# First attention of a two-layer kernel: value projection of one head in full float32 against two heads per product in three rounded passes

## The chip, the cores and the metric

The kernel runs on 1 core of one Trainium2 chip. The metric is the device time of one execution in microseconds (us); the median of several runs is compared.

## The reference, cut to what matters

Two transformer layers over 4 x 256 tokens of width 256; the case is about the first operation, an attention of 16 heads of 128:

```python
q = split_heads(x @ Wq); k = split_heads(x @ Wk); v = split_heads(x @ Wv)
q = _apply_rope(q, cos, sin); k = _apply_rope(k, cos, sin)
scores = einsum('bhqd,bhkd->bhqk', q, k) / sqrt(HD)      # causal mask, softmax
ctx = einsum('bhqk,bhkd->bhqd', attn, v)
return ctx @ Wo
```

After it come a layer norm, a decay scan, a mixture of experts with 32 experts, and the second layer (attention, gated linear attention, experts). Everything is float32.

## The kernel before, in words

Sizes: T = 1024 tokens (B = 4 sequences of S = 256, NT = 8 tiles of 128), D = 256 (DC = 2 chunks of 128 rows), H = 16 heads, HD = 128. The program of each engine is written out by hand; engines meet only at semaphores, and each engine executes its own list strictly in order.

`layer0_attention` (lines 346 to 611) treats one head per round, `heads(emit)`, and in a round the four sequences b = 0..3. Beside the attention of head h, TensorE projects head h + 1. `CHUNKS` names the six projection jobs of a head: q and k and v, each for two halves of 512 tokens; `BESIDE = {0: (0, 1), 1: (2, 3), 2: (4, 5), 3: ()}` puts q0 and k0 into round b = 0, v0 and q1 into b = 1, k1 and v1 into b = 2, nothing into b = 3. All jobs use two PSUM banks in turn (`proj_ps[:, c % 2]`), so each job waits until the job two before it has been read out: a q or k job by VectorE's `rotate_in` (line 488 multiplies by the cosine, line 492 shuffles neighbouring rows; semaphore rot_in), a v job by ScalarE's `keep_v` (line 572; semaphore v_kept).

- q and k jobs go through `product` (lines 72 to 78): weights and tokens are cut into a rounded float32r high part and a low part, and three matmuls (high x low, high x high, low x high) stand for one float32 matmul. The high part of a head's weights is made by ScalarE in `cut_high` (line 578, at b = 0 of head h for head h + 2), the low part by GpSimd in `cut_low` (line 552), for head 1 by VectorE (line 507). x_h and x_l, the two parts of the tokens, are made once (lines 583 and 499).
- A v job (line 434) is 4 token tiles x 2 chunks = 8 plain float32 matmuls of 128 columns, with k.xT (the tokens, float32) as the stationary operand and the head's 128 columns of Wv moving.

TensorE's order in a round of b: the scores of (h, b) (lines 326 and 327), the projection jobs of that b, the transposes of the softmax of two rounds ago (line 265, waits for VectorE's `divide`, lines 297 to 300, semaphore normed), and probabilities times values of three rounds ago (lines 274 and 275). VectorE's order: maxima (line 334), the `rotate_in` of the jobs of this b, `divide` of the round before. ScalarE's order: `exps` (lines 340, 342), `cut_high` if b = 0, `keep_turned` (line 306), `keep_mixed` (line 313), `keep_v`. GpSimd's order per head: `cut_low` for head h + 2 (two operations), then four `rotate`s for head h + 1, each a multiplication by the sine (line 543) and an addition (line 547; semaphore rotated). The scores of b = 0 wait until GpSimd has finished q0 and k0 of their head, those of b = 2 until it has finished q1 and k1.

SyncE loads Wq, Wk and Wv of a head together, 128 KB each (line 395), two heads ahead; the load of head h waits for the v jobs of head h - 2. `load_rest` (constants) and `load_tail` (k.x, the token-major copy of x, 1 MB, and Wo, 2 MB) stand between the loads of heads 1, 2 and 3. k.x is first read in `layer0_tail` (line 759), after the attention.

Of the kernel before, what the change touches and what calls it, by code (L numbers as in the profile page):

```python
# [41 lines left out]
class Memory:  # L42
# [6 lines left out]
    def sb(self, name, shape, dt=F32):  # L49
        return self.stack.enter_context(self.nc.sbuf_tensor(name, shape, dt))  # L50

# [294 lines left out]
def layer0_attention(nc, k, I):  # L346

    with ExitStack() as stack:
        m = Memory(nc, stack)
        ROT = 4  # L350
        w = m.sb("a0_w", [P, 2, 3, DC, HD])
        w_p = Parts(m, "a0_w", [P, 2, 2, DC, HD])
        x_h, x_l = m.sb("a0_x_h", [P, DC, T], F32R), m.sb("a0_x_l", [P, DC, T], F32R)
        qk = m.sb("a0_qk", [P, 2, 2, T])
        v = m.sb("a0_v", [P, 2, NT, HD])
# [8 lines left out]
        w1_low = m.sem("a0_w1_low")  # L364
        w_in = [m.sem("a0_w_in0"), m.sem("a0_w_in1")]
        qk_proj = m.sem("a0_qk_proj")
# [11 lines left out]
        NQK = {0: 1, 1: 2, 3: 3, 4: 4}  # L378
        NV = {2: 1, 5: 2}
# [9 lines left out]
        with nc.Block() as block:  # L389
            @block.sync  # L390
            def _(sp):
                def load(h, par):
                    at_least(sp, v_proj, 2 * (h - 2) + 2)
                    for n, name in enumerate(("L0_attn_Wq", "L0_attn_Wk", "L0_attn_Wv")):
                        sp.dma_start(w[:, par, n], I[name][:, h * HD:(h + 1) * HD].rearrange("(c p) d -> p c d", p=P)
                                     ).then_inc(w_in[par], 16)
                load(0, 0)
                load(1, 1)
                load_rest(sp, k, I)
                load(2, 0)  # L400
# [12 lines left out]
            @block.tensor  # L413
            def _(pe):
                def project(h, pair, par, c):
                    what, half = CHUNKS[c]
                    if what == "v":
                        pe.wait_ge(w_in[par], 48 * (pair + 1))
                    else:
                        if h == 1:  # L420
                            pe.wait_ge(w1_low, PIECE[what] + 1)
                        else:
                            pe.wait_ge(w_low, 2 * max(h - 1, 0) + PIECE[what] + 1)
                    if h == 0:
                        pe.wait_ge(x_low, DC * (half + 1))
                    prev, prev_h = (c - 2, h) if c >= 2 else (c + 4, h - 1)
                    if prev in NQK:
                        at_least(pe, rot_in, 4 * prev_h + NQK[prev])
                    else:
                        at_least(pe, v_kept, 2 * prev_h + NV[prev])  # L430
                    if what == "v":
# [5 lines left out]
                        last.then_inc(v_proj, 1)  # L437
                    else:
                        tokens = slice(half * HALF, (half + 1) * HALF)
                        for kc in range(DC):  # L440
                            last = product(pe, proj_ps[:, c % 2, :], w_p[:, par, PIECE[what], kc, :],
                                           (x_h[:, kc, tokens], x_l[:, kc, tokens]), kc == 0, kc == DC - 1)
                        last.then_inc(qk_proj, 1)

                def mix(h, par, b):
                    if b % 2 == 0:
                        pe.wait_ge(v_kept, 2 * h + b // 2 + 1)
                    at.mix(pe, 4 * h + b, b, lambda j: v[:, par, 2 * b + j, :])
# [3 lines left out]
                for c in range(len(CHUNKS)):  # L452
                    project(0, 0, 0, c)
                pe.wait_ge(k.first_in, k.n_first)

                def emit(h, pair, par, first, last, ahead):
                    for b in range(B):
# [4 lines left out]
                        if not last:  # L462
                            for c in BESIDE[b]:
                                project(h + 1, pair + par, 1 - par, c)
# [15 lines left out]
            def _(dve):  # L480
                def rotate_in(h, c):
                    what, half = CHUNKS[c]
                    count = 4 * h + NQK[c]
                    r = NQK[c] - 1
# [4 lines left out]
                                      proj_ps[:, c % 2, :].rearrange("p (b s) -> p b s", b=2),  # L489
                                      cos[:, None, :].to_broadcast([P, 2, S]), ALU.mult)  # L490

                    dve.stream_shuffle(swapped[:, r, :], proj_ps[:, c % 2, :], [i ^ 1 for i in range(32)]  # L492
# [9 lines left out]
                for c in NQK:  # L502
                    rotate_in(0, c)
# [17 lines left out]
                def emit(h, pair, par, first, last, ahead):  # L521
                    for b in range(B):
                        n = 4 * h + b
                        at.maxima(dve, n, b)
                        if not last:
                            for c in BESIDE[b]:
                                if c in NQK:
                                    rotate_in(h + 1, c)
# [2580 lines left out]
```

## Time and profile before

| | us |
|---|---|
| median of 3 runs | 1132.42 (1131.62 to 1134.52) |
| span of the profiled execution | 1133.0 |
| first projection matmul (q0 of head 0) | at 10.61 |
| scores of head 0 begin | at 20.57 |
| scores of head 15 (the last) begin | at 260.11 |
| output projection of the attention begins | at 276.26 |
| TensorE busy in the span | 1029.7 (91%) |
| VectorE, ScalarE, GpSimd busy | 732.4 (65%), 574.6 (51%), 466.2 (41%) |

Times in the trace are us from the start of the span. PE is TensorE's matmuls, PEld its weight loads, DVE VectorE, ACT ScalarE, POOL GpSimd. A matmul's bar begins when it starts and overlaps the next one, so what a matmul costs is read from the start of one to the start of the next. A float32 matmul stands in the trace as two records, a float32r matmul as one.

### The profile page before, as it was taken

Reading aid. Unit: us, or ns where it says so; the run is one execution under the profiler, and the core shown is the slowest. Engines: PE = TensorE matmul, PEld = TensorE weight load, DVE = VectorE, ACT = ScalarE, POOL = GpSimd, SP = SyncE. Lnnn points to the kernel's source line nnn. Section 1 sums busy time; section 2 is a strip of 40 time slices with the busy share of each in tenths; the row PEclk is TensorE's granted clock in tenths of the full one; section 3 lists DMA queues with packets and bytes.
Section 4 is the critical chain, followed back from the end, with each engine's and each line's share of the span. In section 5 each row is a group of like instructions: output and inputs, shape, how many; then the busy total and the mean of one; then the engine's idle time right before and its main releaser. Section 6 shows DMA issues by size and latency. Waiting matters only on the chain. (4 is left out here: it accounts for less than half of the span.)

```text
span 1133.0 us, 18735 instructions
## 1 busy us (share of the span) xinstructions
PE 1029.7 (91%) x5986; PEld 825.7 (73%) x5986; DVE 732.4 (65%) x2146; ACT 574.6 (51%) x1568; POOL 466.2 (41%) x481
## 2 busy tenths in 40 slices
PE   8999999998995699579899999988978889999995
PEld 5888888887873699547778888845444568877784
DVE  5988887883675366446656672126686657788875
ACT  3454555445221355346667772037875546655553
POOL 5777777861277344455111110010135313444322
PEclk9999999999997899879999999988998989999998
DMA  6631111000011799626101101001003011112101
GB/s 217 235 132 61 29 30 28 19 12 1 1 54 56 237 354 333 196 69 186 37 25 61 30 15 38 1 21 50 2 1 114 0 56 56 57 56 75 38 1 38
DMA packets 83495, 85.59 MB, mean 76 GB/s; under 512 B 8545, under 2 KB 75943, under 8 KB 83280
## 3 DMA queue, kind: packets, MB, share of 16 engines
q1 hardware_dynamic: 79056, 75.39, 20.4%
q0 software_dynamic: 3072, 7.34, 2.2%
q10 hardware_dynamic: 1280, 1.77, 0.5%
q8 instruction: 46, 0.75, 0.3%
q14 instruction: 41, 0.34, 0.1%
HBM read 63.36 MB, written 22.02 MB: 75 GB/s over the span
## 5 line engine op out<-in xcount | busy, mean ns | idle before, releaser
L547 POOL TENSOR_TENSOR a_qk<-h,a_by_sin 128x512 f32<-128x512 f32 x64 | 86.6, 1353 | 5.0
L334 DVE CUSTOM_DVE_ANT_0 h<-a_score_ps,mask_bf 128x128 f32<-128x128 f32 (+1 forms) x128 | 40.7, 355 | 62.0 <-PE a_score_ps L327 62.0
L306 ACT ACTIVATE a_probsT<-a_turn_ps 128x384 f32<-128x384 f32 x128 | 61.3, 479 | 36.1 <-PE a_turn_ps L265 36.1
L1265 POOL TENSOR_TENSOR a_w_l<-a_w,a_w_h 128x256 fp32r<-128x256 f32 x30 | 21.8, 727 | 113.1 <-ACT a_w_h L1458 112.9
L340 ACT ACTIVATE y_moe<-y_moe,a_nmax 128x128 f32<-128x128 f32 x64 | 25.7, 402 | 82.8 <-DVE a_nmax L334 82.5
L434 PEld LDWEIGHTS a_proj_ps<-a_w,xT 128*128 128x128 f32 x512 | 62.0, 192 | 3.2 <-issue 1.2
L434 PE MATMUL a_proj_ps<-a_w,xT 128*128 128x128 f32 x512 | 62.5, 275 | 0.4 <-DVE hT L492 0.4
L1004 POOL TENSOR_TENSOR e_w_l<-e_w,e_w_h 128x512 fp32r<-128x512 f32 x32 | 40.9, 1278 | 52.3 <-ACT e_w_h L1072 52.3
L76 PE MATMUL a_proj_ps<-a_x_l,a_w_h 128*128 128x512 f32 x128 | 55.8, 436 | 2.6 <-ACT a_v L572 0.8
L728 PE MATMUL t_y_ps<-wo,attnT 128*128 128x256 f32 x256 | 57.6, 381 | 0.0
L2513 POOL TENSOR_TENSOR m_up_l<-m_up_w,m_up_h 128x1024 fp32r<-128x1024 f32 x8 | 19.5, 2434 | 89.4 <-ACT m_up_h L2485 89.4
L1505 PE MATMUL p_y_ps<-wo,attnT 128*128 128x256 f32 x256 | 55.5, 379 | 0.8 <-PEq L1237 0.8
L299 DVE TENSOR_SCALAR y_moe<-y_moe,a_rtotal 128x128 f32<-128x128 f32 x64 | 53.4, 835 | 2.3
L1505 PEld LDWEIGHTS p_y_ps<-wo,attnT 128*128 128x128 f32 x256 | 48.6, 190 | 7.5 <-issue 0.9
L728 PEld LDWEIGHTS t_y_ps<-wo,attnT 128*128 128x128 f32 x256 | 47.7, 190 | 6.0
L78 PE MATMUL a_proj_ps<-a_x_h,a_w_l 128*128 128x512 f32 x128 | 50.4, 394 | 0.0
L340 ACT ACTIVATE h<-h,a_nmax 128x128 f32<-128x128 f32 x64 | 25.7, 402 | 48.2 <-DVE a_nmax L334 48.2
L77 PE MATMUL a_proj_ps<-a_x_h,a_w_h 128*128 128x512 f32 x128 | 50.0, 390 | 0.0
L492 DVE STREAM_SHUFFLE hT<-a_proj_ps 128x512 f32<-128x512 f32 x64 | 47.2, 737 | 0.0
L334 DVE CUSTOM_DVE_ANT_0 y_moe<-a_score_ps,mask_bf 128x128 f32<-128x128 f32 (+1 forms) x128 | 40.2, 349 | 9.7 <-PE a_score_ps L327 9.6
L543 POOL TENSOR_TENSOR a_by_sin<-hT,sin_k 128x512 f32<-128x512 f32 x32 | 41.2, 1287 | 10.0 <-DVE hT L492 10.0
L1997 DVE TENSOR_TENSOR wo<-l_dec,l_qk_ps 128x384 f32<-128x384 f32 x64 | 35.2, 550 | 15.6 <-ACT l_dec L1960 14.1
(439 smaller groups left out, 3373.6 us busy)
## 6 DMA issues: line engine op xcount, KB each, us to landing
slots<-zeros SPq DMA_DIRECT2D x4, 2048.0 KB, 7.1
e_rows<-slots SPq DMA_DIRECT2D x32, 256.0 KB, 4.7
e_w<-in_L_ffn_w_dram SPq DMA_DIRECT2D x32, 256.0 KB, 4.9
out_slots<-e_out SPq DMA_DIRECT2D x32, 256.0 KB, 4.3
e_w<-in_L_ffn_w_dram SPq DMA_DIRECT2D x32, 128.0 KB, 4.3
a_w<-in_L_attn_w_q_dram SPq DMA_DIRECT2D x32, 128.0 KB, 2.3
m_up_w<-in_up_dram SPq DMA_DIRECT2D x8, 512.0 KB, 3.8
a_w<-in_L_attn_Wq_dram SPq DMA_DIRECT2D x16, 128.0 KB, 2.3
```

The lines of the kernel that those rows point to most:

```text
L76: pe.matmul(out, left[0], right[1], start=start, stop=False)
L77: pe.matmul(out, left[0], right[0], start=False, stop=False)
L78: return pe.matmul(out, left[1], right[0], start=False, stop=stop)
L299: dve.tensor_scalar(self.probs[:, b, 0:P], self.probs[:, b, 0:P], self.rtotal[:, b, 0:1], None, ALU.mult)
L306: act.activation(self.probsT[:, b % 2, :], self.turn_ps[:, b % 2, 0:CAUSAL], ACT.Copy).then_inc(self.turned_kept, 1)
L334: done = dve.tensor_tensor_reduce(self.probs[:, b, cells], self.score_ps[:, r, cells], self.k.mask_bf[:, cells], -1.0, 3e38, ALU.add, ALU. ...
L340: act.activation(self.probs[:, b, 0:P], self.probs[:, b, 0:P], ACT.Exp, bias=self.nmax[:, b, 0:1], scale=-1.0, accum_out=self.total[:, b, ...
L434: last = pe.matmul(proj_ps[:, c % 2, t * HD:(t + 1) * HD], k.xT[:, kc, half * HALF + t * P:half * HALF + (t + 1) * P], w[:, par, 2, kc, :] ...
L492: dve.stream_shuffle(swapped[:, r, :], proj_ps[:, c % 2, :], [i ^ 1 for i in range(32)]).then_inc(rot_in, 1)
L547: pool.tensor_tensor(qk[:, par, 0 if what == "q" else 1, half * HALF:(half + 1) * HALF], by_cos[:, r, :], by_sin[:, r2, :], ALU.add).then_ ...
L728: last = pe.matmul(y_ps[:, t % 2, 0:D], k.ctxT[:, h, t * P:(t + 1) * P], k.wo[:, h, :], start=h == 0, stop=h == H - 1)
L1505: last = pe.matmul(y_ps[:, t % 2, 0:D], k.ctxT[:, h, t * P:(t + 1) * P], k.wo[:, h, :], start=h == 0, stop=h == H - 1)
```

## The change

Values are no longer projected per head but per group of two heads (VG = 2, eight groups). A value job is now a quarter of the tokens (two tiles of 128) for 256 columns of Wv, in float32r parts, three matmuls for each tile and chunk: 2 x 2 x 3 = 12 matmuls of 256 columns. There are four such jobs per group, two beside each head, at the places where the value jobs stood; the group of heads 2g and 2g + 1 is projected beside heads 2g - 2 and 2g - 1. All four jobs of group 0 stand in the opening, ahead of the first scores; beside head 14 there are no value jobs. The second value buffer is k.xT, which nothing else reads after the opening; the parts of Wv lie in k.x, so the load of k.x moves behind the last value job. The cuts of Wv come with it: one 128x512 operation of ScalarE and one of GpSimd per group (of VectorE for group 1), for groups 2 to 7 in the odd heads 1 to 11, ScalarE's after `exps` of b = 1, GpSimd's between `cut_low` and the first `rotate`. SyncE loads Wv in 256 KB pieces into a single buffer, each after the cut of the piece before it.

```diff
-        w = m.sb("a0_w", [P, 2, 3, DC, HD])
+        w = m.sb("a0_w", [P, 2, 2, DC, HD])
+        wv = m.sb("a0_wv", [P, DC, VG * HD])
+        wv_h, wv_l = (m.at(f"a0_wv_{n}", [P, 2, DC, VG * HD], k.x_at + i * 8 * DC * VG * HD, F32R)
+                      for i, n in enumerate("hl"))
-        v = m.sb("a0_v", [P, 2, NT, HD])
+        v = [m.sb("a0_v", [P, NT, VG * HD]), k.xT[:, :, :].rearrange("p c (t w) -> p (c t) w", w=VG * HD)]
...
-        CHUNKS = [("q", 0), ("k", 0), ("v", 0), ("q", 1), ("k", 1), ("v", 1)]
-        BESIDE = {0: (0, 1), 1: (2, 3), 2: (4, 5), 3: ()}
+        OPENING = [("q", 0, 0), ("k", 0, 0), ("v", 0, 0), ("q", 0, 1), ("k", 0, 1), ("v", 0, 1), ("v", 0, 2), ("v", 0, 3)]
+        def beside(h, b):
+            if h == H - 1:
+                return []
+            g = h // VG + 1
+            values = [("v", g, 2 * (h % VG) + i) for i in range(2)] if g < GROUPS_V else [None, None]
+            jobs = {0: [("q", h + 1, 0), ("k", h + 1, 0)], 1: [values[0], ("q", h + 1, 1)],
+                    2: [("k", h + 1, 1), values[1]], 3: []}[b]
+            return [job for job in jobs if job]
...
             def _(sp):
                 def load(h, par):
-                    at_least(sp, v_proj, 2 * (h - 2) + 2)
-                    for n, name in enumerate(("L0_attn_Wq", "L0_attn_Wk", "L0_attn_Wv")):
+                    at_least(sp, qk_proj, 4 * (h - 2) + 4)
+                    for n, name in enumerate(("L0_attn_Wq", "L0_attn_Wk")):
...
+                def load_v(g):
+                    if g:
+                        low_of(sp, g - 1)
+                    sp.dma_start(wv[:, :, :], I["L0_attn_Wv"][:, g * VG * HD:(g + 1) * VG * HD
+                                                              ].rearrange("(c p) d -> p c d", p=P)).then_inc(wv_in, 16)
                 load(0, 0)
+                load_v(0)
                 load(1, 1)
+                load_v(1)
                 load_rest(sp, k, I)
                 load(2, 0)
-                load_tail(sp, k, I)
+                load_v(2)
+                load_wo(sp, k, I)
                 for h in range(3, H):
                     load(h, h % 2)
+                    if h % VG and (h + 3) // VG < GROUPS_V:
+                        load_v((h + 3) // VG)
...
+                sp.wait_ge(v_proj, B * GROUPS_V)
+                load_x(sp, k, I)
...
-                        for t in range(NT // 2):
-                            for kc in range(DC):
-                                last = pe.matmul(proj_ps[:, c % 2, t * HD:(t + 1) * HD],
-                                                 k.xT[:, kc, half * HALF + t * P:half * HALF + (t + 1) * P],
-                                                 w[:, par, 2, kc, :], start=kc == 0, stop=kc == DC - 1)
+                        for t in range(QT):
+                            cells = slice((QT * i + t) * P, (QT * i + t + 1) * P)
+                            for kc in range(DC):
+                                last = product(pe, out[:, t * VG * HD:(t + 1) * VG * HD],
+                                               (x_h[:, kc, cells], x_l[:, kc, cells]),
+                                               (wv_h[:, of % 2, kc, :], wv_l[:, of % 2, kc, :]), kc == 0, kc == DC - 1)
...
             def _(dve):
+                dve.wait_ge(wv_high, 2)
+                dve.tensor_tensor(wv_l[:, 1], wv[:, :, :], wv_h[:, 1], ALU.subtract).then_inc(wv1_low, 1)
...
             def _(pool):
+                def cut_values(g):
+                    pool.wait_ge(wv_high, g + 1)
+                    pool.tensor_tensor(wv_l[:, g % 2], wv[:, :, :], wv_h[:, g % 2], ALU.subtract).then_inc(wv_low, 1)
                 cut_low(0, 0)
+                cut_values(0)
...
                     if ahead:
                         cut_low(h + 2, par)
+                    if par and (h + 3) // VG < GROUPS_V:
+                        cut_values((h + 3) // VG)
...
             def _(act):
+                def cut_values(g):
+                    act.wait_ge(wv_in, 16 * (g + 1))
+                    at_least(act, v_proj, B * (g - 1))
+                    act.activation(wv_h[:, g % 2], wv[:, :, :], ACT.Copy).then_inc(wv_high, 1)
...
                         if b == 0 and ahead:
                             cut_high(h + 2, pair + 1, par)
+                        if b == 1 and par and (h + 3) // VG < GROUPS_V:
+                            cut_values((h + 3) // VG)
```

A job's bank is now its number in the whole order modulo 2, and it waits for the read-out of the job two before it, as before. In the opening ScalarE cuts the first head's q and k weights once Wq and Wk have landed (it waited for all three matrices), then Wv of group 0, then the second half of the tokens. The product itself keeps its place and its lines move by four (81, 80 and 82 answer to 77, 76 and 78).

## Rows read from the trace of the kernel before

**Rows 1.** The page: busy share of PE; granted TensorE clock in 40 slices.

```profile
PE 1029.7 (91%) x5986; PEld 825.7 (73%) x5986; DVE 732.4 (65%) x2146; ACT 574.6 (51%) x1568; POOL 466.2 (41%) x481
...
PEclk9999999999997899879999999988998989999998
```

**Rows 2.** Busy time by engine of heads 14, 15 and 7.

```profile
core 0: us, PE busy (x) PEld busy (x) DVE busy (x) ACT busy (x) POOL busy (x), PEclk, DMA share, GB/s
...
243.71:260.11 16.40, 15.90 (x103) 14.00 (x102) 14.45 (x40) 7.68 (x26) 10.44 (x9) 1.00 0.01 1
260.11:273.30 13.19, 10.68 (x64) 8.41 (x62) 6.39 (x34) 9.87 (x36) 0.00 (x0) 1.00 0.00 0
131.00:147.11 16.11, 15.99 (x103) 13.93 (x101) 13.27 (x41) 8.49 (x29) 11.93 (x11) 1.00 0.09 25
```

**Rows 3.** Groups of instructions, first 330 us: busy us, mean ns, idle before.

```profile
L434 PE MATMUL a_proj_ps<-a_w,xT 128*128 128x128 f32 x512 | 62.5, 275 | 0.4 <-DVE hT L492 0.4
...
L299 DVE TENSOR_SCALAR y_moe<-y_moe,a_rtotal 128x128 f32<-128x128 f32 x64 | 53.4, 835 | 2.3
...
L552 POOL TENSOR_TENSOR a_w_l<-a_w,a_w_h 128x256 fp32r<-128x256 f32 x30 | 21.3, 731 | 48.3 <-ACT a_w_h L578 48.2
```

**Rows 4.** Timeline of head 7, PE (start us, length us, engine, line, operation).

```profile
131.00 0.39 PE L326 MATMUL a_score_ps<-a_qk 128*128 128x128 f32 x2
...
136.07 1.95 PE L434 MATMUL a_proj_ps<-a_w,xT 128*128 128x128 f32 x16
...
137.77 0.48 PE L76 MATMUL a_proj_ps<-a_x_l,a_w_h 128*128 128x512 f32 x1
...
142.63 1.95 PE L434 MATMUL a_proj_ps<-a_w,xT 128*128 128x128 f32 x16
...
144.41 0.49 PE L265 MATMUL a_turn_ps<-ident,y_moe 128*128 128x128 f32 x3
...
147.11 0.39 PE L326 MATMUL a_score_ps<-a_qk 128*128 128x128 f32 x2
```

**Rows 5.** Timeline of the first experts, PE, float32r products of 256 columns.

```profile
391.42 0.28 PE L76 MATMUL e_up_ps<-e_rowsT_l,e_w_h 128*128 128x256 f32 x1
...
392.14 1.03 PE L1045 MATMUL e_down_ps<-e_w,e_actT 128*128 128x256 f32 x4
```

**Rows 6.** Timeline of head 7, around TensorE's two waits.

```profile
139.44 0.69 DVE L488 TENSOR_TENSOR h<-a_proj_ps,cos_q 128x512 f32<-128x512 f32 x1 [1.77 <-PE a_proj_ps L78]
...
140.41 0.60 ACT L572 ACTIVATE a_v<-a_proj_ps 128x512 f32<-128x512 f32 x1
...
141.13 0.19 PEld L76 LDWEIGHTS a_proj_ps<-a_x_l,a_w_h 128*128 128x128 f32 x1 [0.50 <-issue]
...
144.39 1.36 DVE L299 TENSOR_SCALAR y_moe<-y_moe,a_rtotal 128x128 f32<-128x128 f32 x1
...
145.68 0.34 DVE L300 TENSOR_SCALAR y_moe<-y_moe,a_rtotal 128x256 f32<-128x256 f32 x1
...
146.07 0.31 PEld L265 LDWEIGHTS a_turn_ps<-ident,y_moe 128*128 128x128 f32 x3 [0.26 <-DVE y_moe L300]
```

**Rows 7.** Timeline of head 7, POOL, and ScalarE where the new cut goes.

```profile
134.11 1.42 POOL L552 TENSOR_TENSOR a_w_l<-a_w,a_w_h 128x256 fp32r<-128x256 f32 x2 [3.08 <-ACT a_w_h L578]
...
135.49 1.27 POOL L543 TENSOR_TENSOR a_by_sin<-hT,sin_q 128x512 f32<-128x512 f32 x1
...
139.76 0.49 ACT L306 ACTIVATE a_probsT<-a_turn_ps 128x384 f32<-128x384 f32 x1 [1.08 <-PE a_turn_ps L265]
...
145.75 1.40 POOL L547 TENSOR_TENSOR a_qk<-h,a_by_sin 128x512 f32<-128x512 f32 x1
```

**Rows 8.** Timeline of the opening.

```profile
9.34 0.72 ACT L578 ACTIVATE a_w_h<-a_w 128x256 fp32r<-128x256 f32 x2 [1.71 <-DMA a_w<-in_L_attn_Wv_dram]
...
10.61 0.50 PE L76 MATMUL a_proj_ps<-a_x_l,a_w_h 128*128 128x512 f32 x1 [0.38 <-POOL a_w_l L552]
...
20.57 0.30 PEld L326 LDWEIGHTS a_score_ps<-a_qk 128*128 128x128 f32 x2
```

More of the change, by code:

```diff
@@ L411, in _, with free @@
                                                                        k.zeros.shape[1]])).then_inc(k.zeroed, 16)
+                sp.wait_ge(v_proj, B * GROUPS_V)
+                load_x(sp, k, I)
             @block.tensor
             def _(pe):
-                def project(h, pair, par, c):
-                    what, half = CHUNKS[c]
+                def free(job):
+                    n = number[job]
+                    if n < 2:
+                        return
+                    what, of, i = order[n - 2]
@@ L417, in project @@
                     if what == "v":
-                        pe.wait_ge(w_in[par], 48 * (pair + 1))
+                        pe.wait_ge(v_kept, B * of + i + 1)
                     else:
[L420 to L426, printed above, removed]
@@ L427, in project @@
[L427 to L443 removed]
+                        pe.wait_ge(rot_in, 4 * of + COUNT[what, i])
@@ L461, in emit @@
                                   lambda i, j: qk[:, par, 1, b * S + i:b * S + j])
-                        if not last:
-                            for c in BESIDE[b]:
-                                project(h + 1, pair + par, 1 - par, c)
+                        for job in beside(h, b):
+                            project(job)
                         if b >= at.TURN or not first:
@@ L480, in _, with rotate_in @@
             def _(dve):
[L481 to L484, printed above, removed]
+                def rotate_in(job):
+                    what, h, half = job
+                    count = 4 * h + COUNT[what, half]
+                    r = COUNT[what, half] - 1
                     dve.wait_ge(qk_proj, count)
@@ L501, in _ @@
                 dve.wait_ge(k.first_in, k.n_first)
-                for c in NQK:
-                    rotate_in(0, c)
+                for job in OPENING:
+                    if job[0] != "v":
+                        rotate_in(job)
                 for piece in range(2):
@@ L524, in emit @@
                         at.maxima(dve, n, b)
[L525 to L528, printed above, removed]
+                        for job in beside(h, b):
+                            if job[0] != "v":
+                                rotate_in(job)
                         if b or not first:
@@ L536, in _, with rotate @@
             def _(pool):
[L537 to L540 removed]
+                def rotate(h, what, half, par):
+                    count = 4 * h + COUNT[what, half]
+                    r, r2 = COUNT[what, half] - 1, COUNT[what, half] % 2
                     sin = k.sin_q if what == "q" else k.sin_k
@@ L585, in _ @@
                         cut_high(0, 0, 0)
+                        cut_values(0)
                 cut_high(1, 0, 1)
-                for c in NV:
-                    keep_v(0, 0, c)
+                keep_v(0, 0)
+                keep_v(0, 1)
+                cut_values(1)
+                keep_v(0, 2)
+                keep_v(0, 3)
                 def emit(h, pair, par, first, last, ahead):
@@ L599, in emit @@
                             at.keep_mixed_act(act, n - at.KEEP, b, h - 1)
-                        if not last:
-                            for c in BESIDE[b]:
-                                if c in NV:
-                                    at_least(act, at.mixed, 4 * h - 2 + 2 * CHUNKS[c][1])
-                                    keep_v(h + 1, 1 - par, c)
+                        for job in beside(h, b):
+                            if job[0] == "v":
+                                keep_v(job[1], job[2])
                 heads(emit)
@@ L2991, in build @@
         k = Shared()
+        k.x_at = -(-nc.sbuf_base // 32) * 32
         k.x = m.sb("x", [P, NT, D])
```

82 lines of the change are left out of this document (57 added, 25 removed).

## The prediction

> **What bounds the kernel now.** I read the page first: TensorE is busy for 91% of the span and its granted clock is near full throughout [rows 1]. An average says nothing of one stage, so next the busy times of one head of the first attention, head 7, from its first scores to those of head 8: 16.11 us, of which PE 15.99, DVE 13.27, POOL 11.93, ACT 8.49, at a granted clock of 1.00, the 2.4 GHz level [rows 2]. TensorE bounds this stage, with VectorE and GpSimd not far behind. The timeline of that head then shows where TensorE still stands. Its weight loads pause twice: 0.50 us ahead of k1, which needs the bank that ScalarE's `keep_v` frees (140.41 + 0.60 = 141.01, k1's load at 141.13), and 0.26 us ahead of the transposes of b = 3, which need VectorE's `divide` (145.68 + 0.34 = 146.02, load at 146.07) [rows 6]. All else in the head is TensorE's own list.
>
> **TensorE, beside a head.** Removed: two value jobs of 16 records (512 in all, as the group's count says [rows 3]). The job in b = 1 runs from 136.07 to the start of q1 at 137.77, 1.70 us; that first q1 matmul is about 0.08 longer than its fellows since it follows float32 work, so the job is worth 1.78. The one in b = 2 runs from 142.63 to 144.41, 1.78 us [rows 4]. Added: two jobs of 12 float32r matmuls of 256 columns. The expert stage has just this form, also with the stationary operand changed each time: six of them from 391.42 to 392.14, so 0.72 / 6 = 0.120 us each [rows 5], and a job is 12 x 0.120 = 1.44 us. The saving is 1.78 - 1.44 = 0.34 us a job, 0.68 a head. The matmul count rises by half, the columns per head by as much, but one pass per column replaces the two records of 0.111 us.
>
> How much of it reaches the clock on the wall is a matter of the two waits. The wait ahead of k1 follows the transposes of b = 1 through ScalarE (`keep_turned` at 139.76, `keep_mixed`, `keep_v` at 140.41 [rows 6, 7]); when the job before those transposes is shorter, the whole chain moves, and the wait stays as it is: 0.34 kept. The job in b = 2 stands beside another chain: from the end of q1 VectorE works without a gap, from the first multiplication at 139.44 to the end of `divide` at 146.02 [rows 6], and only then can TensorE transpose. If VectorE takes as long as now, the 0.34 of this job turns into a longer wait. But in this chain two `divide` operations (line 299) last 1.36 us where the group's mean is 0.835 [rows 3, 6]: GpSimd's operations run at the same time. The Trainium skill (SBUF — State Buffer, the single rule) says that VectorE and GpSimd share a port pair under an exclusive lock, held for a whole instruction; the 1.36 us, as long as one GpSimd operation, agree, and by that rule a shifted GpSimd changes each `divide`. GpSimd does shift here (next paragraph), so VectorE's chain hits other phases of it, and the two collisions are already about the worst there are. Bounds per head: 0.34 (VectorE's chain as long as now) and 0.68 + 0.26 = 0.94 (the chain so much shorter that the second wait goes too). I take 0.68, in the middle and TensorE's own term. Over the 14 heads with values beside them: 4.8 to 13.2, taken 9.5 us.
>
> **The cuts of Wv, on ScalarE and GpSimd.** In six odd heads ScalarE gets one 128x512 operation, as long as `keep_v`, 0.60 us [rows 6], between `exps` and `keep_turned`. It is idle there for 1.08 us [rows 7], of which the shorter value job takes 0.34: 0.74 left for 0.60, so nothing, with 0.1 us a head as the bound. Its own load is a head old by then.
>
> GpSimd gets a wait for that operation, and this is the dangerous spot. Today its list in head 7 is: idle for 3.08, `cut_low` 134.11 to 135.53, then four rotations of 2.7 us each (1.27 and 1.40 and gaps), the last addition ending at 145.75 + 1.40 = 147.15 [rows 7]. In an odd head the first rotation now stands behind `cut_values`, which waits for ScalarE: 139.76 - 1.08 = 138.68 for the end of `exps`, plus 0.60, makes 139.3; then 1.3 us of its own (a 128x512 operation of two SBUF inputs [rows 7]) gives 140.6; q0 and k0 are rotated by 140.6 + 2 x 2.7 = 146.0. The scores of head 8 need exactly these, and TensorE would reach them at 147.11 - 0.68 = 146.4 [rows 4]. So it is hidden by 0.4 us; TensorE gets there at 146.2 at the best gain of 0.94, and 0.1 is then still left. q1 and k1 end near 151.4, and the scores of b = 2 that need them start 9 to 10 us into head 8. In head 8, an even one, GpSimd has no new wait and catches up: it starts its cut at 151.4 instead of 150.2 and ends about 163, before the cut of head 9 can begin near 165. VectorE's buffers are four deep, one per job, and none is wanted before a head later. Queued behind the waiting operation is nothing but rotations. Costed at nothing, then.
>
> **Queues.** SyncE issues per two heads 4 + 1 loads instead of 6. In the opening it stands at the second Wv load until GpSimd has cut the first, some 4 us, and with it the constants that the scans want some 30 us later; Wo and k.x are wanted after 276, k.x can be loaded once the last value job, beside head 13, is done, before 243. Nothing.
>
> **The opening.** Four jobs of 1.44 in place of two of 1.78: +2.2 us. ScalarE waited 1.71 us for Wv and then cut the first head's weights at 9.34, and q0 started at 10.61 behind that cut [rows 8]; it now waits for Wk only, issued half a microsecond earlier: -0.3. The added cuts lie beside other work: `cut_values(0)` on ScalarE and GpSimd ends near 12, value job 0 starts near 13.5; VectorE's cut for group 1 (about 1 us) ends before the delayed scores. Scores of head 0 at 20.57 [rows 8] + 1.9 = 22.5. Bounds +1.3 and +2.6.
>
> **Head 14.** Its two value jobs go outright: 3.56 us of TensorE's 16.40 [rows 2], and the wait for `keep_v` with them, 4.0 at most. But VectorE was busy for 14.45 of them; without its collisions (up to 1 us in each of three `divide`s) some 12 remain, and TensorE's transposes follow VectorE closely once no value job lies between. Lower bound 16.40 - 14.8 = 1.6 (VectorE's list back to back, with a start-up). Taken 2.5. Head 15 has no projections before or after (13.19 us [rows 2]) and keeps its time, and so does all that follows.
>
> **The sum.** -9.5 - 2.5 + 1.9 = -10.1 us; best -13.2 - 4.0 + 1.3 = -15.9, worst -4.8 - 1.6 + 2.6 = -3.8. The profiled execution has 1133.0 of span, which is 0.6 above the median of the runs, 1132.4. Prediction: 1132.4 - 10.1 = 1122.3. What a measurement here can tell from no change is about 0.3%, 3.4 us, so faster means below 1129.0.
>
> **Rivals.**
> (A) VectorE becomes the second bound: its chain keeps its 6.6 us, each head gains 0.34 only. For it: the chain has no gap today. Against: the two `divide`s at 1.36 are at their worst phase. Total -4.8 - 2.0 + 1.9 = -4.9, 1127.5. Chance 0.2.
> (B) The chain shortens and the wait at b = 3 disappears: 0.94 a head, -13.2 - 2.5 + 1.9 = -13.8, 1118.6. For it: in odd heads GpSimd is now idle from 135.5 to 139.3, so the `divide` of b = 0 meets nobody. Against: the longer GpSimd tail then meets the `divide` of b = 3 and can delay the next head's maxima. Chance 0.25.
> (C) Slower: GpSimd's wait for ScalarE's cut. If `exps` of b = 1, or the cut behind it, come later than today, all rotations of an odd head come later one for one, and the scores of the next head wait. It has 0.4 us free; to eat the whole 10.1 us in six heads it must be 1.7 + 0.4 = 2.1 us late in each, to be told as slower 2.7 us. At 3 us late it costs 6 x 2.6 = 15.6: 1138. Against: VectorE's maxima and `exps` of b = 1 come earlier with less collision, not later. Chance 0.04.
> (D) The gain isn't there: the three-pass product of 256 columns takes longer in this place than in the experts, say 0.148 us a matmul (12 x 0.148 = 1.78), so heads gain nothing and opening and head 14 about cancel: 1132. It can be, since here it alternates with float32 work and each first matmul costs some 0.08 more; at 0.08 on every job the gain is still 0.26. Chance 0.06.
> The forecast itself has 0.45, with a range of its own from 1119.5 to 1125.5.
>
> **How the numbers follow.** Faster: 0.45 + 0.25 and most of A's 0.2, 0.86. Same: the rest of A, D, and the mild end of C, 0.1. Slower 0.04. The range takes in B with the larger gain in head 14 and A with the worst terms: 1117.0 to 1128.6.
>
> **What would show it.** Right: the product lines with 128x256 outputs from the token parts, 384 matmuls in all, start to start 0.12 us; scores of head 0 near 22.5; head to head 15.4 us instead of 16.11, alike in odd and even heads; scores of head 15 near 250; the pause ahead of k1 still about 0.5 us; TensorE without a wait for rotations. A shows as a wait of the b = 3 transposes for line 300 (new number) of 0.6 us instead of 0.26. B shows as none there. C shows as PE waiting for POOL's addition at the first scores of heads 2, 4, ... 12, and odd heads longer than even ones. The forecast is wrong if head 14 doesn't fall below 15 us, if the opening costs over 3 us, or if anything behind the attention changes its length.

## The result, and the profile after

The changed kernel takes 1138.22 us, the median of 12 runs (1135.41 to 1140.74), against 1133.84 (1129.55 to 1135.92) for the kernel before in 12 runs beside it. The ratio is 1.0038, with a 95% interval of 1.0025 to 1.005: slower by 0.4%, where 1122.3 us and a gain of 0.9% were predicted. The profiled execution took 1136.5 us, of which 1134.7 are its span.

The page of the changed kernel, busy times and granted clock, beside [rows 1]:

```profile
PE 1017.3 (90%) x5858; PEld 812.6 (72%) x5858; DVE 738.2 (65%) x2147; ACT 578.1 (51%) x1576; POOL 477.8 (42%) x488
...
PEclk9999999999997799879999999988998989999998
```

TensorE is busy 12.4 us less, at the same granted clock in all but one of the 40 slices (none of the attention), so its work did shrink; the time did not. The busy times by engine of heads 7, 8, 14 and 15 of the changed kernel, cut from first scores to first scores as in [rows 2], the last one from its first scores to the output projection:

```profile
136.61:151.90 15.29, 15.17 (x95) 13.27 (x93) 11.20 (x41) 8.50 (x27) 8.87 (x9) 1.00 0.12 34
151.90:168.74 16.84, 15.46 (x95) 13.10 (x94) 15.48 (x43) 8.75 (x31) 16.37 (x14) 1.00 0.06 18
248.47:264.32 15.85, 12.78 (x71) 10.22 (x69) 14.59 (x41) 6.64 (x25) 10.42 (x9) 1.00 0.12 40
264.32:279.96 15.64, 13.02 (x80) 10.39 (x79) 6.18 (x33) 11.10 (x37) 0.04 (x1) 1.00 0.00 1
```

The first column behind the times is the head's length. Head 7 is 0.82 shorter than before, head 8 is 0.73 *longer* than the 16.11 of [rows 2]. In both TensorE has the same 95 matmul records to run. The pattern holds throughout: odd heads 3 to 13 take 15.26 to 15.81 us, even heads 4 to 12 take 16.34 to 16.84, where before every one took 16.07 to 16.11. Scores of head 0 begin at 23.30 (before 20.68; here and below the matmul, which starts 0.11 us behind the weight load of [rows 8]), those of head 15 at 264.32 (before 260.11), the output projection at 279.96 (before 276.26): +3.7 us over the attention, the size of the 4.4 between the medians. (The two spans differ by 1.7 only; what follows the attention was 2.0 us shorter in this execution. The change does nothing there, and over all the traces of this case that part takes 852.0 to 857.8 us, in kernels with and without the change.)

Where the 4.2 us to head 15 lie: opening +2.6, head 0 +2.2, head 1 -0.8, head 2 +2.0, heads 3 to 13 together -1.2, head 14 -0.6.

Next, VectorE's and GpSimd's timeline in head 8 of the changed kernel, with ScalarE and TensorE where they wait (idle time before an operation in brackets). Line 303 is the 128x128 multiplication of `divide` (299 before), 304 the 128x256 one (300 before), 604 `cut_low`, 595 and 599 `rotate`:

```profile
156.88 1.44 POOL L604 TENSOR_TENSOR a_w_l<-a_w,a_w_h 128x256 fp32r<-128x256 f32 x2
...
157.59 0.80 DVE L303 TENSOR_SCALAR y_moe<-y_moe,a_rtotal 128x128 f32<-128x128 f32 x1
...
158.28 1.29 POOL L595 TENSOR_TENSOR a_by_sin<-hT,sin_q 128x512 f32<-128x512 f32 x1
158.32 1.40 DVE L304 TENSOR_SCALAR y_moe<-y_moe,a_rtotal 128x256 f32<-128x256 f32 x1
...
159.77 0.31 PEld L269 LDWEIGHTS a_turn_ps<-ident,y_moe 128*128 128x128 f32 x3 [0.29 <-DVE y_moe L304]
...
160.30 0.40 ACT L344 ACTIVATE y_moe<-y_moe,a_nmax 128x128 f32<-128x128 f32 x1 [3.03 <-DVE a_nmax L338]
...
161.83 0.59 ACT L631 ACTIVATE xT<-a_proj_ps 128x512 f32<-128x512 f32 x1
...
162.54 0.19 PEld L80 LDWEIGHTS a_proj_ps<-a_x_l,a_w_h 128*128 128x128 f32 x1 [1.30 <-issue]
...
166.21 1.28 POOL L595 TENSOR_TENSOR a_by_sin<-hT,sin_k 128x512 f32<-128x512 f32 x1
166.27 1.37 DVE L304 TENSOR_SCALAR y_moe<-y_moe,a_rtotal 128x256 f32<-128x256 f32 x1
...
167.70 0.55 PE L269 MATMUL a_turn_ps<-ident,y_moe 128*128 128x128 f32 x3 [0.45 <-DVE y_moe L304]
```

Read it from the top. The short multiplication ends when GpSimd's cut ends (0.80 instead of 0.29 us). GpSimd's next operation then starts ahead of VectorE's next, and the long multiplication lasts until that one ends too (1.40 instead of 0.34). VectorE has lost 1.6 us. The maxima of b = 1 behind it are late, so ScalarE's `exps` start late (3.03 idle), and with them `keep_turned`, `keep_v` and the bank that k1 needs: TensorE's wait ahead of k1 is 1.30, not the 0.50 of [rows 6]. Later line 304 is caught again, and the transposes of b = 3 wait.

Over the whole attention (the first 300 us of the trace) this shows in the waits (us in total, times, longest). Of the changed kernel:

```profile
PEld a_turn_ps L269 <- DVE y_moe L304: 16.8, 18, 2.7
PEld a_proj_ps L80 <- issue: 13.3, 16, 1.8
```

and of the kernel before:

```profile
PEld a_proj_ps L76 <- issue: 7.5, 14, 0.9
...
PEld a_turn_ps L265 <- DVE y_moe L300: 5.3, 17, 0.7
```

11.5 us more behind `divide` and 5.8 more ahead of projection jobs. The groups of the changed kernel (busy us, mean ns of one) show that the long operations moved from one line to the other:

```profile
L303 DVE TENSOR_SCALAR y_moe<-y_moe,a_rtotal 128x128 f32<-128x128 f32 x64 | 40.1, 626 | 2.3
L304 DVE TENSOR_SCALAR y_moe<-y_moe,a_rtotal 128x256 f32<-128x256 f32 x64 | 39.2, 612 | 0.0
```

Before, line 299 had a mean of 835 ns [rows 3] and line 300 one of 441. The sum of both was 81.7 us and is 79.3. VectorE loses no more time to GpSimd than before; it loses it in other places. Of the 128 multiplications 47 lasted over 0.5 us before, 6 of them on line 300; now 58 do, 17 of them on line 304.

### The profile page after: what moved, and what is told of

It is laid out like the page before. It is cut to its first block and busy times, and to the rows that moved or that the text cites. A ratio compares the mean times of both kernels' runs of the same rounds, so it can differ in the third digit from the quotient of the medians.

```text
span 1134.7 us, 18490 instructions
## 1 busy us (share of the span) xinstructions
PE 1017.3 (90%) x5858; PEld 812.6 (72%) x5858; DVE 738.2 (65%) x2147; ACT 578.1 (51%) x1576; POOL 477.8 (42%) x488
## 5 line engine op out<-in xcount | busy, mean ns | idle before, releaser
L595 POOL TENSOR_TENSOR a_by_sin<-hT,sin_k 128x512 f32<-128x512 f32 x32 | 44.8, 1399 | 2.1 <-DVE hT L543 2.1
L595 POOL TENSOR_TENSOR a_by_sin<-hT,sin_q 128x512 f32<-128x512 f32 x32 | 41.3, 1292 | 6.9 <-DVE hT L543 6.9
L278 PE MATMUL a_mix_ps<-a_probsT,v 128*128 128x256 f32 x128 | 38.8, 384 | 3.6 <-ACT a_probsT L310 3.6
L303 DVE TENSOR_SCALAR y_moe<-y_moe,a_rtotal 128x128 f32<-128x128 f32 x64 | 40.1, 626 | 2.3
```

The source lines that it names most:

```text
L595: pool.tensor_tensor(by_sin[:, r2, :].rearrange("p (b s) -> p b s", b=2), swapped[:, r, :].rearrange("p (b s) -> p b s", b=2), sin[:, None ...
```

## The experiments

The expectations name two theories. *Theory P* (phase): in the odd heads GpSimd's new wait moves its rotations some 5 us later, VectorE's `divide` waits for whatever operation GpSimd is running, and so the same collisions fall at other moments, for better or worse. *Theory W* (work): the added operations themselves, GpSimd's 1.3 us or ScalarE's, do the harm, wherever they stand. Beside them stands a third, rival C's: the rotations come too late for the scores.

**1. GpSimd's cut behind the rotations (late_cut).**

```diff
-                    if par and (h + 3) // VG < GROUPS_V:
-                        cut_values((h + 3) // VG)
                     if not last:
                         for what, half in COUNT:
                             rotate(h + 1, what, half, 1 - par)
+                    if par and (h + 3) // VG < GROUPS_V:
+                        cut_values((h + 3) // VG)
```

> The changed kernel with one move: in odd heads GpSimd cuts the next group's Wv after the four rotations instead of ahead of them, so the rotations wait for nothing new. Theory P (phase): the change is slow in the even heads because GpSimd's rotations stand 5 us later and its operations meet VectorE's divide and scans; then the even heads 4 to 12 fall from 16.3 to 16.8 us to 15.3 to 15.8, head 2 from 18.4 to about 16.2, and the whole is 5 to 9 us faster than the changed kernel, at or a little below the kernel before. Theory W (work): it is the 1.3 us of added GpSimd work or ScalarE's added operation, not where they stand; then even heads stay above 16.2 and the total within 2 us of the changed kernel.

Measured: 1148.52 us, ratio 1.0161 [1.0138, 1.0185], slower still. But the run tests two things. SyncE loads the next piece of Wv only after GpSimd's cut of the one before, and the next head's Wq and Wk stand behind that in its list. The wait of the Wv load, of this kernel:

```profile
SPq L430 <- POOL a_wv_l L609: 114.2, 6, 24.2
```

and what ScalarE and TensorE then wait for in head 4 (20.2 us long; head 2, with 20.6, shows the same), in its timeline:

```profile
104.46 0.72 ACT L638 ACTIVATE a_w_h<-a_w 128x256 fp32r<-128x256 f32 x2 [6.76 <-DMA a_w<-in_L_attn_Wk_dram]
...
105.98 1.19 PE L278 MATMUL a_mix_ps<-a_probsT,xT 128*128 128x256 f32 x2 [3.52 <-ACT attnT L317]
```

In the changed kernel the load's wait is 70.0 us in all and 14.7 at most, and behind the opening nobody waits for Wk. So the 5 to 9 us of gain that were expected can't be judged here, and this run says nothing on the theories; it shows that the order of the queue was not free to be moved past.

**2. The same with the load moved back (late_cut2).** On top of the diff above:

```diff
                     load(h, h % 2)
-                    if h % VG and (h + 3) // VG < GROUPS_V:
-                        load_v((h + 3) // VG)
+                    if h % VG == 0 and (h + 2) // VG < GROUPS_V:
+                        load_v((h + 2) // VG)
```

> The late cut again, with the load of the next Wv piece moved one place back in SyncE's list, behind the q and k weights of the following head, which in the first try stood behind a load that waited for the late cut. Theory P: odd heads 15.3, even heads 15.4 to 16.0 (GpSimd's cut of 1.3 us can still meet VectorE at the head's start), total 1128 to 1133. If even heads stay above 16.2, GpSimd's added work does the harm and not its wait.

Measured: 1138.93 us, 1.0056 [1.0032, 1.0081], no better than the changed kernel and 6 us above the expected range. Even heads 4 to 10 take 16.6 us, odd ones 15.8, and the sum of both `divide` lines, 98.6 us, is the largest of all runs:

```profile
L303 DVE TENSOR_SCALAR y_moe<-y_moe,a_rtotal 128x128 f32<-128x128 f32 x64 | 50.5, 789 | 2.3
L304 DVE TENSOR_SCALAR y_moe<-y_moe,a_rtotal 128x256 f32<-128x256 f32 x64 | 48.1, 752 | 0.0
```

The rotations no longer stand behind ScalarE's cut, and the loss stays: the wait is not the whole of it. By its own words the expectation would put the harm down to GpSimd's added work; runs 3 and 4 take the two apart.

**3. The wait alone, in the kernel before (before_wait).**

```diff
                     if ahead:
                         cut_low(h + 2, par)
+                    if par and h < 12:
+                        pool.wait_ge(at.exped, 4 * h + 2)
                     if not last:
```

> The kernel before with one wait and no work added: in the six odd heads 1 to 11 GpSimd waits, between its cut and its first rotation, for ScalarE's exps of b = 1, the same place at which the changed kernel's cut of Wv waits. Theory P: this alone makes the even heads slower, by 0.4 to 1.2 us each, and the whole by 3 to 8 us. Theory W: the rotations have slack, nothing moves by more than 1 us.

Measured: 1139.92 us, 1.0064 [1.0048, 1.008]. Even heads 4 to 10 take 17.12 to 17.15 us instead of 16.1, head 2 takes 17.95 instead of 16.42; odd ones take 16.03, and head 12, behind the last wait, keeps its 16.1. Head 6 of this kernel, its windows row and its timeline:

```profile
117.41:134.53 17.12, 16.11 (x102) 13.91 (x101) 16.39 (x43) 8.61 (x31) 13.55 (x12) 1.00 0.10 29
```

```profile
123.32 1.27 POOL L543 TENSOR_TENSOR a_by_sin<-hT,sin_q 128x512 f32<-128x512 f32 x1
...
123.36 1.37 DVE L300 TENSOR_SCALAR y_moe<-y_moe,a_rtotal 128x256 f32<-128x256 f32 x1
...
127.28 1.36 DVE L299 TENSOR_SCALAR y_moe<-y_moe,a_rtotal 128x128 f32<-128x128 f32 x1
...
128.56 1.39 DVE L300 TENSOR_SCALAR y_moe<-y_moe,a_rtotal 128x256 f32<-128x256 f32 x1
...
131.83 1.35 DVE L299 TENSOR_SCALAR y_moe<-y_moe,a_rtotal 128x128 f32<-128x128 f32 x1
...
133.50 0.31 PEld L265 LDWEIGHTS a_turn_ps<-ident,y_moe 128*128 128x128 f32 x3 [1.27 <-DVE y_moe L300]
```

Four long operations in a head that had two, and VectorE busy for 16.39 of 17.12 us. TensorE waits nowhere in this attention for a rotation. A wait on an engine that keeps nobody waiting costs the next head 1.0 us in four heads of six, through another engine's durations. Theory W, by which nothing moves, is out here, since this kernel has no added work.

**4. The work taken out, the wait kept (tiny_cut).** GpSimd's cut of groups 2 to 7 is 8 columns wide instead of 256; this leaves out nearly all of the low part of Wv for heads 4 to 15.

```diff
-                    pool.tensor_tensor(wv_l[:, g % 2], wv[:, :, :], wv_h[:, g % 2], ALU.subtract).then_inc(wv_low, 1)
+                    cells = slice(0, VG * HD if g < 2 else 8)
+                    pool.tensor_tensor(wv_l[:, g % 2, :, cells], wv[:, :, cells], wv_h[:, g % 2, :, cells], ALU.subtract
+                                       ).then_inc(wv_low, 1)
```

> The changed kernel with GpSimd's cut of Wv for groups 2 to 7 shrunk from 256 columns to 8 of each chunk, its wait kept; most of the low part of these values is left out. The rotations of an odd head still stand 3.7 of the 5 us late. Theory P: the even heads stay long, above 16.0 on the mean, total 1132 to 1138, though the exact collisions fall differently. Theory W (work): even heads fall to 15.3, total below 1129.

Measured: 1142.38 us, 1.0083 [1.0052, 1.0113]; even heads 4 to 10 take 16.61, odd ones 15.87 where theory W expected 15.3 for the even ones, lines 303 and 304 at means of 751 and 769 ns. Less work for GpSimd is no gain: its rotations stand at yet another moment, and in head 8 five of the eight multiplications last 1.20 to 1.40 us, where in the changed kernel two do.

**5. The lock taken away (noport_after).** If `divide` also writes the sum of its result into an unused column, it should no longer share a port with GpSimd. The Trainium skill (SBUF — State Buffer, who interferes with whom) says that `tensor_scalar` can take the shared pair, but not in the form that also writes out its accumulator.

```diff
+        more = {}, {}
+        if self.row is not None:
+            more = tuple({"op1": ALU.add, "accum_out": self.row[:, b, i:i + 1]} for i in range(2))
+        scalar2 = None if self.row is None else 0.0
-        dve.tensor_scalar(self.probs[:, b, 0:P], self.probs[:, b, 0:P], self.rtotal[:, b, 0:1], None, ALU.mult)
+        dve.tensor_scalar(self.probs[:, b, 0:P], self.probs[:, b, 0:P], self.rtotal[:, b, 0:1], scalar2, ALU.mult,
+                          **more[0])
...
```

> The changed kernel with VectorE's two divide operations of the first attention written in the form that also sums its row (the sum is not used), which by theory P does not contend with GpSimd's operations. Theory P with the port as its means: both operations last 0.3 to 0.5 us wherever GpSimd stands, TensorE's waits for divide go, the even heads fall to 15.3 to 15.7, head 0 to about 13, the whole to 1124 to 1130. If GpSimd's lateness acts otherwise (rotations too late for the scores), even heads stay above 16.2.

Measured: 1122.21 us, 0.9912 [0.9894, 0.993]. The groups and the windows of heads 7, 8 and 14 of this kernel:

```profile
L310 DVE TENSOR_SCALAR_CACHE_REDUCE y_moe<-y_moe,a_rtotal 128x256 f32<-128x256 f32 x64 | 30.4, 475 | 0.0
...
L308 DVE TENSOR_SCALAR_CACHE_REDUCE y_moe<-y_moe,a_rtotal 128x128 f32<-128x128 f32 x64 | 22.2, 346 | 2.3
```

```profile
128.94:144.25 15.31, 15.19 (x95) 13.27 (x93) 11.84 (x50) 8.96 (x29) 9.87 (x9) 1.00 0.12 36
144.25:159.55 15.30, 15.18 (x94) 13.27 (x93) 12.21 (x50) 8.36 (x28) 14.84 (x13) 1.00 0.06 18
236.09:249.04 12.95, 12.31 (x71) 10.39 (x69) 11.43 (x52) 7.16 (x27) 9.18 (x9) 1.00 0.19 67
```

Odd and even heads are alike at 15.3 us, although GpSimd still waits for ScalarE's cut and still carries the long tail into the even head (14.84 us busy there). Both added operations are still in this kernel too, so theory W is out for it. The timeline of head 8 at the same place as above:

```profile
148.99 1.43 POOL L610 TENSOR_TENSOR a_w_l<-a_w,a_w_h 128x256 fp32r<-128x256 f32 x2
149.70 0.35 DVE L308 TENSOR_SCALAR_CACHE_REDUCE y_moe<-y_moe,a_rtotal 128x128 f32<-128x128 f32 x1
...
149.97 0.48 DVE L310 TENSOR_SCALAR_CACHE_REDUCE y_moe<-y_moe,a_rtotal 128x256 f32<-128x256 f32 x1
...
150.38 1.29 POOL L601 TENSOR_TENSOR a_by_sin<-hT,sin_q 128x512 f32<-128x512 f32 x1
...
154.02 0.19 PEld L80 LDWEIGHTS a_proj_ps<-a_x_l,a_w_h 128*128 128x128 f32 x1 [0.50 <-issue]
```

GpSimd runs as before beside `divide` (`cut_low` until 150.4, then the rotation), both multiplications take their own 0.35 and 0.48, and the wait ahead of k1 is 0.50 again.

**6. Is it only a better `divide`? (noport_before, noport_before_wait).** The same diff in the kernel before, and in run 3.

> The kernel before with the same form of divide as the last-but-one experiment, nothing else. Theory P: its two long divides per head (1.36 us) go too, so TensorE's wait ahead of the transposes of b = 3 (0.26 us) goes, heads fall from 16.11 to about 15.85, head 14 from 16.4 to below 16, the whole by 3 to 6 us, to about 1128. The change on top of it is then worth what TensorE's list says, 0.5 to 0.7 us a head and head 14, 5 to 8 us net. If instead the divide's form is what made the changed kernel fast, both come out alike near 1122.

> The kernel before with GpSimd's wait at exps of b = 1 in the odd heads (which by itself made it 0.64% slower) and the divide in its other form. If the wait does its harm only through the divide that meets GpSimd, it costs nothing now: heads 16.0 as in the kernel before with that divide, but for head 2 and the heads with a decay scan, up to 1 us in all; whole within 2 us of 1132. If GpSimd's rotations come too late for the scores, or in any other way, even heads stay near 17.1 and the whole near 1138.

Measured: noport_before 1132.13 us, 0.9994 [0.9973, 1.0015]; its heads take 16.02 to 16.05 us. noport_before_wait 1132.57 us, 0.9986 [0.9969, 1.0003]; its heads take 16.02 us, all but head 2 with 17.02. So GpSimd's wait, which cost 1.0 us in each of the even heads 4 to 10, costs nothing there once `divide` is out of the lock.

The other `divide` is worth hardly anything to the kernel before (0.07 us a head), where 3 to 6 us were expected. Its 0.26 of [rows 6] is a pause of the weight loads; the matmuls of the scores still run meanwhile. From the start of those matmuls to the start of the transposes it takes 0.67 us with the pause (145.40 to 146.07 in head 7) and 0.66 in noport_before, where the load doesn't pause (144.73 to 145.39).

Head 2 shows that the lock itself is still there. Its VectorE operation of 128x2048, the square of the decays, isn't part of `divide`. It takes 2.28 us in noport_before and noport_keep, where head 2 takes 16.0 and 14.9 us like its neighbours, but 3.25 and 3.20 in noport_before_wait and noport_after, where head 2 is 1.0 and 0.9 us longer than they are. In noport_before_wait it starts while GpSimd's addition runs:

```profile
50.74 1.29 POOL L553 TENSOR_TENSOR a_qk<-h,a_by_sin 128x512 f32<-128x512 f32 x1
...
50.92 3.25 DVE L520 TENSOR_TENSOR cT<-cT 128x2048 f32<-128x2048 f32 x1
```

With `divide` out of the lock the change is worth what the traces of noport_before and noport_after say: the output projection at 264.69 instead of 274.77, -10.1 us.

**7. The opening (short_opening, noport_short).** Only two value jobs of group 0 stay ahead of the first scores, the other two go beside head 0.

```diff
-        OPENING = [("q", 0, 0), ("k", 0, 0), ("v", 0, 0), ("q", 0, 1), ("k", 0, 1), ("v", 0, 1), ("v", 0, 2), ("v", 0, 3)]
+        OPENING = [("q", 0, 0), ("k", 0, 0), ("v", 0, 0), ("q", 0, 1), ("k", 0, 1), ("v", 0, 1)]
...
+            if h == 0:
+                return [[("q", 1, 0), ("k", 1, 0)], [("v", 0, 2), ("q", 1, 1)], [("k", 1, 1), ("v", 0, 3)],
+                        [("v", 1, 0), ("v", 1, 1)]][b]
```

> The changed kernel with only two value jobs of group 0 in the opening, the other two beside head 0 (b = 1 and b = 2), and group 1's first two at b = 3 of head 0. The same work in all. If the four opening jobs cost what they take of TensorE because everything waits for the first scores, the first scores come at 20.3 to 20.7 instead of 23.3, and as head 0 has over 3 us of TensorE waits that can take the work in, the scores of head 1 come 1.5 to 3 us sooner: whole 1.5 to 3 us faster than the changed kernel. If head 0 is bound by TensorE, its length grows by the 2.8 us and nothing is gained.

> The divide in its other form and the short opening together. With VectorE out of GpSimd's way head 0 is bound by TensorE, which has all the value jobs to do in either place; the opening ends 2.3 to 2.8 us sooner and head 0 gets as much longer, less the gaps of the long opening (1.43 us ahead of its first value job). Expected 0 to 2 us faster than the divide alone, 1120 to 1122.

Measured: short_opening 1136.39 us, 1.0032 [1.0015, 1.0048], not to be told from the changed kernel; scores of head 0 at 21.04, but that head now takes 17.44. noport_short 1124.35 us, 0.9916 [0.989, 0.9942]: scores at 20.46, head 0 16.97, output projection at 265.61, 0.9 later than without. Of the 1.5 to 3 us expected of short_opening its trace shows 0.4 (output projection at 279.56), and noport_short is no faster than noport_after at all. What leaves the opening comes back in head 0: in noport_short the one is 2.8 us shorter, the other 4.0 longer.

**8. The last wait of TensorE (noport_keep).** With `divide` out of the lock the wait ahead of k1 is 0.50 us in each head; here ScalarE reads the value job out right behind `exps` of b = 1, ahead of `keep_turned`.

```diff
+                        for job in beside(h, b):
+                            if job[0] == "v" and b == 1:
+                                keep_v(job[1], job[2])
                         if b >= at.TURN or not first:
                             at.keep_turned(act, n - at.TURN, (b - at.TURN) % B)
...
-                            if job[0] == "v":
+                            if job[0] == "v" and b != 1:
```

> The changed kernel with the other divide, and ScalarE copying the value job of b = 1 out of its bank right after exps, ahead of keep_turned and keep_mixed. TensorE's wait ahead of k1, 0.50 us a head, is the one left; it goes if nothing else stands behind it, and the 14 heads take 14.8 to 15.0 instead of 15.3: 4 to 7 us, about 1116. If VectorE's chain of this head is the next bound the gain is under 2 us. Over ScalarE the added 0.6 us ahead of keep_turned can delay the odd heads by 0.3.

Measured: 1116.7 us (1111.49 to 1118.54), 0.9844 [0.9815, 0.9873]. Heads take 14.89 to 14.96 us, the output projection begins at 258.78. This version beats both kernels: 0.4 us a head over noport_after, about the size of the wait (0.50, now gone from these heads), at the place where the prediction had left it standing.

## Why the prediction was wrong

Slower had been given 4 in 100, and 1138.22 lies above the range. Point by point:

- **TensorE's term was right.** In the value job of head 7 there are nine matmuls from the start at 141.93 to the one at 142.99 (TensorE's timeline below), 0.118 us each (0.120 forecast), and rival D is out. Without the lock, heads 0 to 13 are 9.0 us shorter in all (221.85 to 212.84 us, noport_before against noport_after), where 9.5 was taken; with it odd heads still get 0.3 to 0.8.

```profile
141.93 0.28 PE L82 MATMUL a_proj_ps<-a_wv_h,a_x_l 128*128 128x256 f32 x1
...
142.99 0.28 PE L82 MATMUL a_proj_ps<-a_wv_h,a_x_l 128*128 128x256 f32 x1
```

- **"the two collisions are already about the worst there are" is the step that failed**, and with it the bounds "per head: 0.34 (VectorE's chain as long as now) and 0.68 + 0.26 = 0.94". They bounded VectorE's chain below by "as long as now" and had no end for longer. In head 7, of eight multiplications only three were lengthened, two to 1.36 us (one of them in [rows 6]) and one to 0.78, each the short one of a pair. The worst is every one caught, two in a row at that. Head 8 of the changed kernel shows two in a row, and head 14 of the kernel before had them already, so its own trace could have told:

```profile
248.77 1.32 DVE L299 TENSOR_SCALAR y_moe<-y_moe,a_rtotal 128x128 f32<-128x128 f32 x1
...
250.01 1.39 DVE L300 TENSOR_SCALAR y_moe<-y_moe,a_rtotal 128x256 f32<-128x256 f32 x1
```

Heads 3 to 13 gave 1.2 us in place of 7.5 (11 x 0.68), heads 0 and 2 lost 2.2 and 2.0. The text had even said that "a shifted GpSimd changes each `divide`", and then let the shift go only one way. The other end of the range was too good as well: the "0.26" of the second wait, counted whole in 0.94, is worth 0.07 us a head (noport_before).
- **"the wait stays as it is: 0.34 kept" failed by the same cause.** It took the chain ahead of k1 to hang on the transposes alone. Their neighbour in ScalarE's list, `exps` of b = 1, hangs on VectorE's maxima, which stand behind `divide`. The wait was 1.30 us in head 8.
- **"Costed at nothing" for GpSimd's wait** held for what it priced (no scores wait for a rotation) and failed for what it did not. The price of the shift was in VectorE's durations: 1.0 us in each of the even heads 4 to 10 in before_wait, nothing in noport_before_wait. Rival C named the place, and gave its chance to a mechanism that never showed: TensorE did not wait for rotations. Its 1138 agrees with the result by accident.
- **Head 0 was costed like the other 13, at 0.68,** though no row of it was read. It lost 2.2 us, against a gain of 0.4 (13.38 to 13.02) without the lock. Head 2, costed the same, lost 2.0; VectorE's square stands there and took 3.38 us instead of 2.28.
- **Head 14:** 2.5 taken, 0.55 measured, 3.1 without the lock (16.02 to 12.94). VectorE was busy for 14.59 of its 15.85 us; "without its collisions some 12 remain" came true in noport_after only (11.43).
- **The opening:** 1.9 taken, 2.6 measured, the upper bound. The timeline of the opening shows the first value job waiting for VectorE's read-out of q0, which stands behind its cut of the tokens. That cut overlaps GpSimd's new `cut_values(0)` and took 2.34 us, where it took 1.79 before; the job started at 14.41 instead of "near 13.5", although q0 itself began 0.6 us earlier than before (9.97), not 0.3:

```profile
10.57 1.29 POOL L609 TENSOR_TENSOR a_wv_l<-a_wv,a_wv_h 128x512 fp32r<-128x512 f32 x1
10.67 2.34 DVE L550 TENSOR_TENSOR a_x_l<-xT,a_x_h 128x512 fp32r<-128x512 f32 x2 [2.45 <-ACT a_x_h L648]
...
14.41 0.35 PE L80 MATMUL a_proj_ps<-a_wv_l,a_x_h 128*128 128x256 f32 x1 [1.43 <-DVE hT L543]
```

- **Head 15** "keeps its time": its stretch to the output projection got 0.5 us shorter (16.15 to 15.64), with and without the lock. The cause stays open.

With `divide` out of the lock the sum is met, -10.1 us in the traces, but that it is met to the tenth is luck: the terms are off and cancel (opening +2.5, heads 0 to 13 -9.0, head 14 -3.1, head 15 -0.5). The error is the term that the lock was given on the loss side: none. One of the prediction's own signs of being wrong showed in the profile (head 14 not below 15 us), and three of its signs of being right were missing (odd and even heads alike at 15.4, the pause ahead of k1 still at 0.5, head 15 at 250 instead of 264).

What stays open: which phase a head falls into could not be read from the trace of before, and no run took GpSimd's work away altogether. VectorE's scans still collide in noport_after (1.58 and 1.08 us in turn, 0.69 alone), yet its heads 3 to 13 all take 15.3 us, so there they cost nothing.

## What to carry to other kernels

When two engines lengthen each other's operations, a change that shifts one of them has no one-sided bound: take as the loss side every short operation of the critical one lasting as long as the other's longest, twice in a row where two follow each other, before you call a moved wait free. In the timeline such a pair is told by one and the same operation having two durations; find a form of it that doesn't contend first, and only then judge, or make, changes to the rest. Here that form was worth nothing by itself, and turned a change that cost 0.4% into one that gains 0.9%.

## What the runs showed of the hardware

- A VectorE `tensor_scalar` on 128x128 or 128x256 f32 takes 0.29 or 0.34 us alone and up to 1.38 or 1.43 (changed kernel) when a GpSimd `tensor_tensor` runs: it ends just behind that operation. In these traces the engine that has stood waiting goes next: in head 8 VectorE's first multiplication was let in between two operations of GpSimd, and its second stood behind the other of them: 0.5 and 1.06 us lost in a row. The Trainium skill (SBUF — State Buffer, who interferes with whom) calls this an exclusive lock for a whole instruction, in which the order of issue decides who blocks, and the traces agree.
- It works the other way too. In head 2 of the changed kernel VectorE's square of 128x2048 waited for GpSimd's addition to end and took 3.38 us (2.28 alone), and GpSimd's multiplication, which had begun at 56.20, waited for the square: 3.31 instead of 1.28.

```profile
54.81 1.42 POOL L599 TENSOR_TENSOR a_qk<-h,a_by_sin 128x512 f32<-128x512 f32 x1
55.00 3.38 DVE L568 TENSOR_TENSOR cT<-cT 128x2048 f32<-128x2048 f32 x1
56.20 3.31 POOL L595 TENSOR_TENSOR a_by_sin<-hT,sin_k 128x512 f32<-128x512 f32 x1
```

- VectorE's scan of 128x256 contends as well, here beside GpSimd's addition and, in the same kernel, alone:

```profile
152.49 1.43 POOL L599 TENSOR_TENSOR a_qk<-h,a_by_sin 128x512 f32<-128x512 f32 x1
...
152.68 1.78 DVE L572 TENSOR_TENSOR_SCAN cT<-decay,cT 128x256 f32<-128x256 f32 x1
...
169.11 0.68 DVE L572 TENSOR_TENSOR_SCAN cT<-decay,cT 128x256 f32<-128x256 f32 x1
```

- The form with an accumulator was never lengthened in the five runs that use it (345 to 351 ns with 128 columns, 472 to 480 with 256, over all of them): each of its 128 multiplications in noport_after took 0.34 to 0.35 us (128 columns) or 0.47 to 0.48 (256 columns). Start to start that is 0.27 us (149.70 to 149.97) in place of 0.20 (149.51 to 149.71 in the changed kernel) for the short one.
